# Shorter tile heads, narrower frame copies and another order of the blocks in a displaced 3x3 convolution

## The reference

```python
x = x + _L0_conv_ref(_gn(x), L0_conv_offset)        # _gn: group norm, 32 groups of 24 channels

off_px = offset * SCALE                             # SCALE = 64
off_int = round(off_px); sub = off_px - off_int
shifted = x moved by off_int, zero where it leaves the image
kx = fx + sub_x; ky = fy + sub_y                    # fx, fy in -1, 0, 1
kern = exp(-(kx*kx + ky*ky) / (2 * SIGMA * SIGMA))  # SIGMA = 0.5
kern = kern / kern.sum()
out = 3x3 convolution of shifted, one kernel per channel, padding 'SAME'
```

## Time and profile before

| | |
|---|---|
| median of 3 runs | 976.3 us (976.01 to 976.35) |
| the profiled execution | 979.06 us, of which the span in the profile is 977.1 us |
| DMA | 403.09 MB, mean 413 GB/s |
| PE, DVE, ACT, POOL busy | 785.6, 824.8, 638.9, 368.1 us |
| chain that ended last | DVE 28%, DMA 27%, PE 20%, POOL 7% |

### The profile page before, as it was taken

How to read it: one execution, slowest core, us unless ns; L and a number is a source line. 1 busy time by engine, 2 the same in 40 slices (tenths; PEclk the granted TensorE clock), 3 DMA queues, 4 the chain that set the end, 5 groups by cost and what they waited for, 6 DMA issues and landing times.

```text
span 977.1 us, 9088 instructions
## 1 busy us (share of the span) xinstructions
PE 785.6 (80%) x2132; PEld 383.6 (39%) x2132; DVE 824.8 (84%) x551; ACT 638.9 (65%) x461; POOL 368.1 (38%) x348
## 2 busy tenths in 40 slices
PE   0998987979979698897979879689797997979820
PEld 0544443434434343353434434345343443434410
DVE  7587988777798997978889899898998979797795
ACT  7778676564766747678466746577675785774661
POOL 0214034340432624013254393463845438250312
PEclk9999988989979799897998979989898897989955
DMA  9999999999999999999999999999999999999948
GB/s 364 427 401 423 392 405 429 429 429 428 430 429 430 432 428 414 430 429 430 431 429 406 398 433 376 407 419 393 431 408 430 430 427 431 431 431 430 430 208 343
DMA packets 27821, 403.09 MB, mean 413 GB/s; under 512 B 3216, under 2 KB 3216, under 8 KB 3216
## 3 DMA queue, kind: packets, MB, share of 16 engines
q1 hardware_dynamic: 27792, 402.71, 98.0%
HBM read 201.38 MB, written 201.33 MB: 412 GB/s over the span
## 4 chain that ended last, share of the span: by engine, by line
DVE 28%; DMA 27%; PE 20%; POOL 7%; issue 7%; ACT 5%; DVEq 3%; ACTq 2%; SPq 0%; POOLq 0%
PE sum_ps L289 17%; DMA out_dram<-xs 15%; DMA xs<-x_dram 12%; DVE xs L713 6%; DVE xs L716 6%; DVE smooth L709 6%; DVE smooth L704 6%; DVE xs L719 4%; POOL small L253 2%; POOL small L260 2%; ACT frame L417 2%; POOL small L257 2%; ACT unused L484 2%; POOL small L266 1%; ACTq L393 1%
## 5 line engine op out<-in xcount | busy, mean ns | idle before, releaser
L289 PE MATMUL sum_ps<-xs,bands 128*128 128x512 f32 x976 | 483.5, 653 | 51.2 <-DMA xs<-x_dram 51.2
L484 ACT ACTIVATE unused<-xs,small 128x4096 bf16 (+1 forms) x94 | 348.3, 3706 | 8.3 <-ACT small L470 4.8
L417 ACT ACTIVATE frame<-xs,small (+1 forms) x96 | 223.3, 2326 | 184.3 <-DVE smooth L709 183.3
L289 PEld LDWEIGHTS sum_ps<-xs,bands 128*128 128x128 f32 x976 | 200.6, 210 | 295.4 <-issue 282.2
L253 POOL TENSOR_TENSOR small<-small 128x3 f32<-128x3 f32 x32 | 41.6, 1299 | 570.6 <-ACT small L492 570.6
L289 PE MATMUL sum_ps<-xs,halves 128*128 128x512 f32 x496 | 230.0, 619 | 17.4 <-DMA xs<-x_dram 17.4
L704 DVE SCALAR_TENSOR_TENSOR smooth<-frame,side_w 128x612 f32 (+5 forms) x96 | 163.6, 1705 | 72.2 <-ACT frame L417 37.1
L713 DVE SCALAR_TENSOR_TENSOR xs<-smooth,small,xs 128x612 f32 (+5 forms) x96 | 163.5, 1703 | 51.9 <-POOL small L266 49.6
L709 DVE SCALAR_TENSOR_TENSOR smooth<-frame,side_w,smooth x96 | 159.7, 1664 | 7.5 <-DVE smooth L704 4.1
L719 DVE SCALAR_TENSOR_TENSOR xs<-smooth,small,xs 128x594 f32 (+9 forms) x96 | 159.8, 1664 | 3.4
L716 DVE SCALAR_TENSOR_TENSOR xs<-smooth,small,xs 128x594 f32 (+9 forms) x96 | 159.7, 1664 | 3.4
(11 more groups left out here) (132 smaller groups left out, 259.3 us busy)
## 6 DMA issues: line engine op xcount, KB each, us to landing
xs<-x_dram SPq DMA_DIRECT2D x96, 2048.0 KB, 14.8
out_dram<-xs SPq DMA_DIRECT2D x96, 2048.0 KB, 17.7
smooth<-offset_dram SPq DMA_DIRECT2D x1, 48.0 KB, 4.1
```

Of the source, the lines that this page charges most:

```text
L289: last = nc.tensor.matmul(sum_ps[:, :], (FIRST, SAME, SECOND)[i], slot_px(n, c * BANK, (c + 1) * BANK), start=(i == 0 and c == 0), stop=(i ...
L417: nc.scalar.activation(frame[:, bass.ds(b, rows * PITCH)].rearrange("p (r c) -> p r c", c=PITCH)[:, :, LEFT:LEFT + W], xs[:, bass.ds(a, ro ...
L484: nc.scalar.activation(unused[:, :], xs[:, bass.ds(n % SLOTS * PIX, PIX)], ACT.Square, bias=neg_mean[:, i:i + 1], accum_out=squares[:, i:i ...
```

## The change

Three things change.

The order of the blocks, `PAIRS`. Which tiles stand next to each other changes, and nothing in the order of the instructions.

The head of a tile on DVE: a fifth word, `BESIDE`, is made in the setup, and `turn` and `behind` are worked out between lines 704 and 709 in place of before line 704. The loop counts from 1, so that `n` and `n + 1` are one register (`side_w` gets a column more).

The copies on ACT: where at most 34 columns are needed, a copy is 34 columns wide, at column 0 or 30, and has 64 rows for a 64 or 50 row tile, and 34 rows for a 34 or 18 row tile. There are six variants of the copy in place of four. The table `fills` moves into the upper 64 partitions of `words`.

```diff
-    PAIRS = [(9, 4), (3, 13), (5, 0), (7, 2), (10, 14), (8, 1), (6, 11), (12, 15)]
+    PAIRS = [(12, 1), (10, 15), (8, 14), (7, 13), (6, 11), (5, 2), (3, 4), (9, 0)]
...
+    WORDS = 5
+    KIND, TO, FROM, BESIDE, COLUMN = range(WORDS)
+    NARROW = 2
+    COPIES = [(rows, W) for rows in SIDES] + [(SIDES[k], SIDES[NARROW]) for k in (0, NARROW)]
+    COL_BITS = (W - SIDES[NARROW]).bit_length()
...
-                    rows = SIDES[k]
+                    rows, cols = COPIES[k]
...
                     nc.scalar.activation(
-                        frame[...].rearrange("p (r c) -> p r c", c=PITCH)[:, :, LEFT:LEFT + W],
-                        xs[:, bass.ds(a, rows * W)].rearrange("p (r c) -> p r c", c=W),
+                        frame[...].rearrange("p (r c) -> p r c", c=PITCH)[:, :, LEFT:LEFT + cols],
+                        xs[:, bass.ds(a, rows * W)].rearrange("p (r c) -> p r c", c=W)[:, :, 0:cols],
...
                 dve.reg_load(next_tile, words[0:1, bass.ds(done * WORDS, WORDS)])
+                turn = kind_of % 2
+                behind = (src + 1 - turn).with_bounds(min_val=1, max_val=most + 1)
...
-                dve.reg_mov(at_turn, kind_of & 1)
-                dve.reg_mov(at_behind, src + 1 - turn)
-                dve.reg_mov(at_beside, src + 2 * turn - 1)
+                beside = dve.snap(next_tile[BESIDE], min_val=0, max_val=FRAME_ROWS * PITCH)
...
-            with dve.Fori(0, TILES) as n:
+            with dve.Fori(1, TILES + 1) as n:
```

More of the change, by code:

```diff
@@ L104, in build @@
         base_w = xs[:, SLOTS * PIX:].rearrange("p (n k) -> p n k", k=3)
-        side_w = [sb(f"side_w{k}", [P, TILES]) for k in range(2)]
+        side_w = [sb(f"side_w{k}", [P, TILES + 1]) for k in range(2)]
         words = sb("words", [P, WORDS * (TILES + 1)], i32)
-        fills = sb("fills", [P, TILES], i32)
+        fills = words[HALF:P, 0:TILES]
         setup = smooth[:, 0:11 * 2 * POSITIONS].rearrange("p (n f a) -> p n f a", n=11, a=2)
@@ L404, in fill_frame @@
                 act.reg_mov(frames, u * UT + i)
-                act.reg_mov(copy_from, base + row * W)
-                act.reg_mov(copy_to, row * PITCH + PAD * PITCH)
+                act.reg_mov(copy_from, base + row * W + column)
+                act.reg_mov(copy_to, row * PITCH + column + PAD * PITCH)
+                source = act.snap(copy_from, min_val=0, max_val=SLOTS * PIX)
+                target = act.snap(copy_to, min_val=PAD * PITCH, max_val=FRAME_ROWS * PITCH)
+                done = act.snap(frames, min_val=1, max_val=TILES)
                 if i == 0:
@@ L680, in _, with smooth_tile @@
             V.engine_nop().then_inc(tile_done, 1)
-            next_tile = [dve.alloc_register(name) for name in ("next_kind", "next_to", "next_from", "next_column")]
+            next_tile = [dve.alloc_register(name) for name in
+                         ("next_kind", "next_to", "next_from", "next_beside", "next_column")]
             done_count = dve.alloc_register("done_count")
-            at_turn, at_beside, at_behind = (dve.alloc_register(name) for name in ("turn", "beside", "behind"))
-            def smooth_tile(rows, cols, src, beside, behind, turn, dst, n, done, weights):
+            def smooth_tile(rows, cols, src, beside, kind_of, most, dst, done, weights):
                 under = xs[:, bass.ds(dst, rows * W)]
@@ L700, in smooth_tile @@
                 sm = smooth[:, 0:rows * cols].rearrange("p (r c) -> p r c", c=cols)
-                part = smooth[:, bass.ds(turn, rows * cols)].rearrange("p (r c) -> p r c", c=cols)[:, :, 0:cols - 1]
                 dve.wait_ge(frame_ready, done)
-                V.scalar_tensor_tensor(sm, frame_window(beside, cols), side_w[0][:, bass.ds(n, 1)], frame_window(src, cols),
+                V.scalar_tensor_tensor(sm, frame_window(beside, cols), side_w[0][:, bass.ds(done, 1)], frame_window(src, cols),
                                        ALU.mult, ALU.add
@@ L708, in smooth_tile @@
                 dve.reg_load(next_tile, words[0:1, bass.ds(done * WORDS, WORDS)])
-                V.scalar_tensor_tensor(part, frame_window(behind, cols - 1), side_w[1][:, bass.ds(n, 1)], part,
+                turn = kind_of % 2
+                behind = (src + 1 - turn).with_bounds(min_val=1, max_val=most + 1)
+                part = smooth[:, bass.ds(turn.with_bounds(min_val=0, max_val=1), rows * cols)].rearrange(
+                    "p (r c) -> p r c", c=cols)[:, :, 0:cols - 1]
+                V.scalar_tensor_tensor(part, frame_window(behind, cols - 1), side_w[1][:, bass.ds(done, 1)], part,
                                        ALU.mult, ALU.add
@@ L741, in emit @@
                     smooth_tile(rows, cols, src.with_bounds(min_val=1, max_val=most),
-                                beside.with_bounds(min_val=0, max_val=most + 1),
-                                behind.with_bounds(min_val=1, max_val=most + 1), turn,
+                                beside.with_bounds(min_val=0, max_val=most + 1), kind_of, most,
                                 dst.with_bounds(min_val=0, max_val=(SLOTS - 1) * PIX + (H - rows) * W + W - cols),
-                                n, done, weights)
+                                done, weights)
                 choose(dve, kind_of, 0, len(SIDES) ** 2, emit, 2)
```

67 lines of the change are left out of this document (39 added, 28 removed).

## The result

The changed kernel takes 1013.97 us (median of 4 runs, 1002.8 to 1016.25), the one before 976.15 beside it (4 runs, 973.61 to 976.35). The ratio is 1.037, with an interval of 1.029 to 1.045. It is 38 us slower; forecast were 9.5 us less. The profiled execution is 1014.98 us, its span 1012.9, against 979.06 and 977.1 before.

What follows compares the result with a forecast made beforehand. The DMA bounds the kernel, its queue busy 98.0% of the span, about 40 us lost. Winning 8.0 us in the middle and 1.5 in the tail takes 9.5 off the median 976.3: 966.8 us; range 958.5 to 975.

Steps and rivals of the forecast that it cites:

- the head of a tile: In front of tiles on DVE: 0.39 us less where DVE waits for its sequencer; three a pass, 1.2 us.
- the head's rival: Head of a tile: bundle behind line 704 and longer register load give the gain back; 971 us, chance 0.08.
- The slower rival: Passes 3 to 6: DMA's reserve of queued work never forms, SP waits for tiles; 981.2 us, chance 0.08.
- under 415 GB/s in passes 3 to 6: DMA rate in the passes of (10, 15) and (8, 14) that would show the forecast wrong.
- start: First two passes: DMA loss stays at 5.7 us, with bounds of 3 us either way.
- heavy passes: Four passes of (10, 15) and (8, 14): DMA loses 1.0 us in sum, far bound 8.4; 58.5 us long.
- (5, 2): Two passes of blocks 5 and 2: 60.2 us each, DMA loses 3.4 us over both, bounds 0 and 6.
- tail: DVE's last units, blocks 12 and 9: 1.5 us won, bounds 0 and 3.
- The copies: Narrower copies on ACT: shorter DVE waits, priced at 0, bound 2 us won.
- No wait for weights by POOL: Last unit: line 713 waiting over 2 us for POOL would show it wrong; POOL's step up to 1.0 us longer.

Runs made afterwards that it cites:

- e1: Changed kernel with four-word register loads at multiples of 16 bytes, COLUMN a stepped register (the four-word kernel): 969.9 us, ratio 0.9947 to the kernel before.
- e3: Kernel before, each load taking a fifth, unused word, rows still 16 bytes apart: 983.87 us, ratio 1.0081.
- e4: Kernel before, four-word loads from a table moved by one word, so starting 4 bytes behind a multiple of 16: 1011.8 us, ratio 1.0373.
- e2: Kernel before with the new block order PAIRS alone: 973.43 us, ratio 0.9978.
- e5: Four-word version of the changed kernel with the old block order PAIRS: 973.55 us, ratio 0.9970.
- e6: Four-word version of the changed kernel with every copy 64 columns wide again: 971.51 us, ratio 0.9956.
- e9: Kernel before, four-word loads from a table moved by two words, so starting 8 bytes behind a multiple of 16: 1014.45 us, ratio 1.0392.
- e10: Kernel before, five-word loads from a table moved by one word, every start off a multiple of 16: 1069.45 us, ratio 1.0942.
- e7: Changed kernel, still five words, with the load moved behind the second of a tile's five operations: 1058.78 us, ratio 1.0848 to the kernel before.

## Why the prediction was wrong, point by point

**The step that failed.** It is the head of a tile: the sum has no term for the register load that the change lengthens and moves. The prediction said that the bundle behind line 704 is "covered by that operation unless it is very short" and priced the fifth word at nothing, without a reason; only the head's rival named "the longer register load", as something that could at most give back 0.39 us a tile, and put that at 971. No row of the load stood among the rows, though the row was to be had: 340/590/1336 ns. It shows a load of four words whose median is already longer than the first operation of an 18x18 tile (556 ns). What the runs put in the place of that nothing is 44 us between the changed kernel and the same with a four-word load (e1), 7 for the word and 35 for the start when either stands alone (e3, e4). That should have made the load a term with a lower and an upper bound. A fifth word at the rate of the four is 0.15 us (590 / 4); measured are 0.24 us in the minimum and 0.6 us in the mean, 7 us in the end. The 35 us of the start (e4) followed from no row of before. What could be seen was that `words` changed its stride from 16 to 20 bytes, and that its cost was unknown.

By the Trainium skill (Runtime: NRT & Kernel Launch, Instruction fetch mechanics) a register load takes some 200 ns a register; the page speaks of the runtime's own loads, from HBM. The loads here come from SBUF and don't follow it: four words take at least 340 ns at a multiple of 16 bytes and 961 off it, so that the number of registers alone doesn't set the time.

**The sign.** The slower rival, a reserve that never forms in passes 3 to 6, at 981, was another mechanism and far too small. The sign "under 415 GB/s in passes 3 to 6" did come, and the gaps of DVE say why: not heavy tiles, but the load. Windows of the kernel after (columns as in the earlier trace rows), the four heavy passes and two lighter ones:

```profile
150.30:213.10 62.80, 52.66 (x139) 25.99 (x138) 53.94 (x30) 36.28 (x29) 34.09 (x20) 0.89 0.96 392
213.10:276.00 62.90, 50.19 (x134) 24.93 (x133) 53.96 (x30) 37.18 (x29) 32.71 (x20) 0.86 0.98 397
276.00:342.00 66.00, 55.53 (x150) 26.87 (x148) 53.65 (x30) 39.04 (x30) 28.37 (x21) 0.92 0.99 411
342.00:403.50 61.50, 47.98 (x131) 23.44 (x130) 53.65 (x31) 35.41 (x28) 29.46 (x22) 0.89 0.97 395
403.50:463.10 59.60, 49.78 (x133) 24.31 (x132) 50.83 (x31) 36.33 (x27) 22.72 (x19) 0.89 1.00 413
...
587.60:646.50 58.90, 47.47 (x129) 23.48 (x129) 50.00 (x30) 36.10 (x28) 30.95 (x22) 0.86 0.99 410
```

DVE's work is what the prediction counted (53.8, 53.7, 50), and around it stand 7.9 to 12.4 us where it had 5.0 less 1.2. Passes of 50 us of work lose now too. In the four-word kernel these two passes run at 427 and 429. That is the mark of something that every pass pays.

**The other steps**, which can be read in the four-word kernel, since there the load is as before. Its windows, start, heavy passes, (5, 2) and tail:

```profile
32.30:88.60 56.30, 55.52 (x179) 28.70 (x178) 48.61 (x30) 42.71 (x34) 20.46 (x21) 1.00 0.98 404
88.60:141.40 52.80, 43.90 (x114) 20.64 (x113) 48.67 (x31) 35.27 (x27) 25.84 (x20) 0.90 1.01 412
141.40:201.30 59.90, 53.31 (x150) 25.94 (x148) 53.96 (x31) 36.17 (x29) 28.95 (x20) 0.89 1.01 431
201.30:261.10 59.80, 52.05 (x144) 25.74 (x143) 53.95 (x30) 37.09 (x29) 32.99 (x20) 0.89 1.01 430
261.10:321.20 60.10, 52.17 (x138) 25.30 (x139) 53.67 (x30) 39.06 (x30) 29.63 (x21) 0.89 1.01 427
321.20:380.30 59.10, 49.44 (x135) 23.62 (x133) 53.64 (x31) 35.37 (x28) 30.36 (x20) 0.91 1.01 427
...
616.80:677.70 60.90, 51.16 (x138) 24.56 (x139) 55.33 (x31) 37.22 (x28) 23.99 (x21) 0.92 1.00 412
677.70:738.50 60.80, 51.63 (x139) 24.73 (x138) 55.26 (x30) 37.00 (x28) 25.12 (x22) 0.89 1.00 415
...
912.20:960.70 48.50, 12.92 (x45) 8.34 (x44) 42.02 (x31) 21.58 (x17) 14.18 (x20) 0.64 0.74 315
960.70:967.80 7.10, 0.00 (x0) 0.00 (x0) 0.04 (x1) 0.00 (x0) 0.00 (x0) 0.50 0.70 295
```

- The start was to stay at 5.7: it loses 56.3 x 26/430 + 52.8 x 18/430 = 5.6.
- The four heavy passes were to lose 1.0 and run at 427 or more: they lose 0.8, at 427 to 431. The length was off, 59.1 to 60.1 for 58.5; that the DMA lost so little even so is presumably the reserve. It isn't the order alone that does it: in e2, with the old head and wide copies, the same four passes lose 4.8.
- (5, 2) was to lose 3.4 and loses 2.6 + 2.1 = 4.7.
- The tail was to win 1.5. The last pass loses 48.5 x 115/430 = 13.0 for 16.2, so 3.2 are won. From the last DVE operation to the end are 7.1 us for 7.4.
- The sum was a span of 967.6; measured is 967.8. With errors of +1.3 and -1.7 in it that is luck in part, and more of it is luck in the execution it started from: the profiled one of before lay 2.8 above its median, the one of e1 on its own. By the medians the four-word kernel wins 6.7 us and not 9.5. Most of the 9.5 was put down to the new order, which is worth 3.2 (e2) to 4.2 (e1 less e5).
- The head: gaps ahead of the first operation were to shrink by 0.3 to 0.4 at light tiles. The eight 18x18 tiles have 2.2 us of them in both kernels for 4.3, 0.27 a tile. But the bundle isn't covered as the prediction said: even with four words the idle time ahead of the second operation is 19.4 us for 7.5. What the head wins is then e6 against e2, 971.51 and 973.43, each by its ratio: 0.2% or 2 us, which their intervals don't tell from nothing.
- The copies were priced at 0 with a bound of 2 won: 1.6 in the medians. Line 427 has 183.9 us for 223.3 in the page. "At about half" holds only for the narrow copies of 64 row tiles (2.1 us for 3.7); those of 34 row tiles take 1.3 for 2.1, of 50 row tiles 2.1 for 3.0, and of 18 row tiles 1.3 as before.
- No wait for weights by POOL: line 745 of the last unit waits 0.68 us in the four-word kernel, under the 2 that would have shown the tail wrong. POOL's first step there takes 2.31 us:

```profile
942.81 2.31 POOL L257 TENSOR_TENSOR small<-small 128x3 f32<-128x3 f32 x1 [20.31 <-ACT small L500]
945.23 0.34 POOL L261 TENSOR_SCALAR small<-small 128x1 f32<-128x1 f32 x1
```

for 1.78; its DVE neighbours take 2.8 us for 1.16. That is 0.5 longer, and the step behind it, whose neighbour is short, takes 0.34. The trace agrees with the rule of the Trainium skill that the prediction weighed (GPSIMD Engine Reference, Key points: POOL contends with DVE instructions of two SBUF inputs). The other units show it more strongly: in the kernel before, the 32 first steps of POOL (line 253) take from 0.86 to 3.97 us, and beside the longest DVE's operations of a tile run for 3.86 us.

**The range.** 958.5 to 975 held the four-word kernel and not the changed one. It was built from the DMA's losses and had no term for DVE's sequencer, though the change touched the load and the bundles in its loop. A bound for the load, from its own row of before, would have been there: if every load took the longest, 1336 for a median of 590 ns, the three light tiles a pass that the head's term counted would give 48 x 0.75 = 36 us of DVE time. That is an estimate and no forecast, but a range with it goes beyond 976.

**What is open.** The minimum of a load goes 340, 580, 961 and 1181 ns, by the word and by the start. The mean lies 0.25 to 1.6 us above that, and single loads up to 4 us. That stretch goes with the tile's place in its unit. In e4 the median load is 1178 ns beside a unit's first tile, 1589 beside the second and 2408 beside the third; in e9 and e10 the order is the same, and the aligned four-word loads of the kernel before have no such order (means of 627, 560 and 575). POOL is busy for 75%, 46% and none of the time of those loads in e4, so that the long ones stand where POOL rests; the PE, ACT and DMA shares show no such trend. No run tells why. The late load (e7) suggests too that the place of a load matters. What was measured is that the time of the kernel follows the word and the start.

## What to carry to other kernels

A register load from a table in SBUF stands in the engine's own path: in the changed kernel the second operation of a tile waited for it. Give its row to the sum like that of any operation, and look at what it must fit under: here the first operation of the lightest tile. When a table of words grows, keep each row at a multiple of 16 bytes from its start, or make the extra word by register arithmetic: one `reg_mov` in place of the word turned 1014 us into 970. Five words with every row at a multiple of 16 were run in the kernel before only (e3, 7 us slower).

If every pass loses the same, look for what every tile pays, before looking at the heavy ones.

## What the runs showed of the hardware

- A load of four words from SBUF into DVE's registers took at least 340 ns when its start was a multiple of 16 bytes from the table's and 961 or 962 when it was 4 or 8 bytes behind one; of five words 580 and 1181 (4 behind).
- The same load's duration spread widely inside one run: 594 to 4952 ns in the changed kernel.
- The same microsecond of load costs more the longer the loads already are: 57 us more of them in all cost 7 us in e3, 118 us more cost 35 in e4, and 74 more on top of that (from e4 to e10) cost 58.
- Steps of POOL of the same form took 0.86 us, and up to 3.97 with DVE's operations of two SBUF inputs beside them (line 253, kernel before).
